# Joining the fourth sequence's last two products on TensorE at the turn, and sharing six indices of the third sequence instead of five

## What is computed

```python
def step(state, inp):
    dt_t, B_t, C_t, u_t = inp
    dA = jnp.exp(dt_t[..., None] * A)                       # (b, 2048, 16)
    state = state * dA + (dt_t * u_t)[..., None] * B_t[:, None, :]
    y = jnp.einsum('bdn,bn->bd', state, C_t)                # sum over the 16 indices n
    return (state, y)
_, ys = jax.lax.scan(step, init, xs)
y = ys.transpose(1, 0, 2) + x * D
y = y * jax.nn.silu(gate)
return y @ W_out.T
```

## Time and profile before

| | us |
|---|---|
| median of 3 runs | 2993.81 (2993.78 to 2994.83) |
| the profiled execution | 2995.75 |
| its span, first to last instruction | 2993.6 |
| PE / DVE busy | 2732.6 / 2552.1 |
| ACT / POOL busy | 1692.0 / 1925.1 |
| mean granted TensorE clock | 0.963 |

### The profile page before, as it was taken

How to read it: one execution, slowest core, us unless ns; L and a number is a source line. 1 busy time by engine, 2 the same in 40 slices (tenths; PEclk the granted TensorE clock), 3 DMA queues, 4 the chain that set the end, 5 groups by cost and what they waited for, 6 DMA issues and landing times.

```text
span 2993.6 us, 35283 instructions
## 1 busy us (share of the span) xinstructions
PE 2732.6 (91%) x11120; PEld 1562.5 (52%) x11120; DVE 2552.1 (85%) x3521; ACT 1692.0 (57%) x2848; POOL 1925.1 (64%) x884
## 2 busy tenths in 40 slices
PE   8968899999989999998999888788889999999996
PEld 4535555555555555555555455455544555555553
DVE  2259899999999999999999999999966787787785
ACT  2356566575656657565565755656534555555553
POOL 1159897888979788896988988889841222222221
PEclk9989899999999999999999999898999999999998
DMA  5432333434343343424333322432401211111110
GB/s 176 134 101 81 97 88 104 147 89 129 92 134 114 99 143 90 132 85 157 94 108 104 99 87 73 133 86 65 118 29 37 97 56 56 63 56 56 63 63 22
DMA packets 132876, 281.32 MB, mean 94 GB/s; under 512 B 12528, under 2 KB 12656, under 8 KB 132224
## 3 DMA queue, kind: packets, MB, share of 16 engines
q1 hardware_dynamic: 132736, 279.59, 30.4%
HBM read 245.86 MB, written 33.69 MB: 93 GB/s over the span
## 4 chain that ended last, share of the span: by engine, by line
PE 54%; DVE 31%; issue 9%; ACT 4%; POOL 1%; DMA 0%; DVEq 0%; ACTq 0%; POOLq 0%; SPq 0%
DVE arena L1262 17%; PE banks L473 15%; PE banks L497 9%; DVE arena L1278 7%; PE banks L567 7%; PE banks L707 4%; PE banks L660 4%; PE banks L616 3%; PE banks L641 3%; PE banks L510 2%; PE banks L671 2%; PE banks L631 2%; ACT banks L1023 2%; DVE arena L1218 1%; PE banks L714 1%
## 5 line engine op out<-in xcount | busy, mean ns | idle before, releaser
L1186 POOL TENSOR_TENSOR arena<-arena 128x2048 f32<-128x2048 f32 x256 | 1161.8, 4539 | 79.8 <-PE banks L567 79.7
L1262 DVE TENSOR_TENSOR_SCAN arena<-banks,arena 128x512 f32<-128x512 f32 x1024 | 1185.4, 1205 | 19.2 <-POOL arena L1186 16.2
L1023 ACT ACTIVATE banks<-arena,a_sb 128x508 f32<-128x508 f32 x1024 | 696.9, 684 | 734.5 <-DVE arena L1262 734.1
L473 PE MATMUL banks<-arena 128*128 128x512 f32 x2048 | 952.9, 603 | 11.0 <-DMA arena<-in_xT 8.1
L567 PEld LDWEIGHTS banks<-ident,arena 128*128 128x128 f32 x4096 | 493.6, 146 | 418.6 <-issue 197.7
L567 PE MATMUL banks<-ident,arena 128*128 128x128 f32 x4096 | 576.2, 284 | 139.4 <-DVE arena L1278 72.6
L473 PEld LDWEIGHTS banks<-arena 128*128 128x128 f32 x2048 | 373.1, 195 | 363.8 <-issue 360.5
L1278 DVE SCALAR_TENSOR_TENSOR arena<-banks,cg,arena 128x512 f32<-128x512 f32 x640 | 453.0, 739 | 72.4 <-PE banks L567 71.6
L497 PE MATMUL banks<-arena 128*128 128x512 f32 x1024 | 472.3, 600 | 5.2 <-DMA arena<-in_WoutT 3.9
L1132 POOL TENSOR_TENSOR arena<-arena 128x512 f32<-128x512 f32 x240 | 306.0, 1275 | 205.3 <-ACT arena L851 204.1
L1199 POOL TENSOR_TENSOR arena<-arena 128x512 f32<-128x512 f32 x128 | 141.2, 1103 | 434.6 <-DVE arena L1434 434.5
(11 more groups left out here) (137 smaller groups left out, 2977.1 us busy)
## 6 DMA issues: line engine op xcount, KB each, us to landing
arena<-b_scratch SPq DMA_DIRECT2D x128, 512.0 KB, 5.1
arena<-in_WinX SPq DMA_DIRECT2D x128, 256.0 KB, 2.9
arena<-in_WinZ SPq DMA_DIRECT2D x128, 256.0 KB, 2.7
arena<-in_WoutT SPq DMA_DIRECT2D x32, 1024.0 KB, 5.8
u_scratch<-arena SPq DMA_DIRECT2D x64, 256.0 KB, 5.1
arena<-u_scratch SPq DMA_DIRECT2D x16, 1024.0 KB, 9.3
arena<-x_scratch SPq DMA_DIRECT2D x32, 512.0 KB, 3.4
arena<-in_xT SPq DMA_DIRECT2D x14, 1024.0 KB, 7.9
```

The lines of the kernel that those rows point to most:

```text
L473: last = nc.tensor.matmul(home(kind, i), wr[w % 2][:, k, :], x[:, k, :], start=(k == 0), stop=(k == KC - 1))
L1023: nc.scalar.activation(by_seq(bank(i % 2))[:, :, 1:SEQ], by_seq(dt[s % 2][:, i, :])[:, :, 1:SEQ], ACT.Exp, scale=a_sb[:, QD * q + i, n:n + ...
L1186: nc.gpsimd.tensor_tensor(hb[n % 4].rearrange("p (i t) -> p i t", i=QD), dtu, brep[pair % 3][:, n % 2:n % 2 + 1, :].broadcast_to([P, QD, G ...
L1262: nc.vector.tensor_tensor_scan(h, bank(i % 2), h, 0.0, ALU.mult, ALU.add)\
```

## The change

`SHARED` gets six indices instead of five, (0, 3, 6, 8, 10, 12) for (0, 3, 6, 9, 12): VectorE makes ten products of sequence 2 per step where it made eleven, ScalarE six and GpSimd five adds for it where they were five and four. GpSimd adds sequence 3's products of indices 1 to 13 alone (SUMS = 13, where it was 15). Those of 14 and 15 stay in the two buffers of `part`; the turn waits for ScalarE's products of all 16 indices and for 13 sums, and where it transposed `acc[:, OWN, :]` it now runs three matmuls with the identity that add `acc[:, OWN, :]`, `part[:, 0, :]` and `part[:, 1, :]` in PSUM.

```diff
-SHARED = (0, 3, 6, 9, 12)
+SHARED = (0, 3, 6, 8, 10, 12)
+SUMS = N - 3
@@ pe_step, behind the loop over n
             pe.wait_ge(S["acc_ok"], KEPT * (s + 1))
-            pe.wait_ge(S["sum_ok"], (N - 1) * (s + 1))
+            pe.wait_ge(S["part_ok"], N * (s + 1))
+            pe.wait_ge(S["sum_ok"], SUMS * (s + 1))
             pe.wait_ge(S["sum2_ok"], (len(SHARED) - 1) * (s + 1))
@@
-                for b in (0, 1, OWN):
+                for b in (0, 1):
                     nc.tensor.transpose(y[:, b * P:(b + 1) * P], acc[:, b, i * P:(i + 1) * P], ident[:, :])
+                for k, v in enumerate((acc[:, OWN, :], part[:, 0, :], part[:, 1, :])):
+                    nc.tensor.matmul(y[:, OWN * P:GB * P], v[:, i * P:(i + 1) * P], ident[:, :], start=(k == 0),
+                                     stop=(k == 2))
@@ act_part
-                after(act, "sum_ok", (N - 1) * s + max(n - 2, 0))
+                after(act, "sum_ok", SUMS * s + max(n - 2, 0))
@@ pool_sums
-            if n == 0:
+            if n == 0 or n > SUMS:
                 return
             pool.wait_ge(S["part_ok"], N * s + n + 1)
-            after(pool, "sum_ok", (N - 1) * s + n - 1)
+            after(pool, "sum_ok", SUMS * s + n - 1)
```

## The result

The median of the changed kernel is 3005.99 us (3003.53 to 3006.64, 8 runs), that of the kernel before in the same comparison 2993.80: a ratio of 1.0038 with a 95% interval of 1.0029 to 1.0046, +12.2 us. The forecast was slower, 3007, so +13.2 against the 2993.81 it started from, with 2996 to 3014 as its range. The profiled execution has a span of 3004.9 us where the kernel before has 2993.6.

The account below looks back on a forecast made before the run. TensorE and VectorE were both taken as full, with TensorE setting each step's turn. Terms 7.8 - 0.5 + 0.2 + 5.5 + 0.6 = +13.6 us on the profiled 2995.75 gave 3009.3, as a median 3007, range 2996 to 3014.

Parts of the forecast that it names:

- 1, 2, 5, 6, 9: Full steps whose turn delays the next step's n = 1, where VectorE waits for TensorE: +1.3 us each.
- 4, 8: Steps followed by the layer norm on VectorE, in whose wait TensorE's +1.3 vanishes: -0.5 us for both.
- 10 to 15: Step 10 as a full step, +1.3 us; steps 11 to 15, late steps without convolution tiles from 11 on, +5.5 together.
- The matmuls: At the turn, 20 more TensorE records at 0.109 us each, covered by nothing: +2.18 us per turn.
- The wait ahead of the turn: TensorE's wait for GpSimd's last add goes: -0.53 us per full step; step 0 waited 5.06 us there.
- The bank of the second tile: Second of the turn's four banks waits for VectorE's L1291 once TensorE is early: gives back about 0.3 us.
- The sixth index: VectorE product fewer, n = 8 to 11: -0.65 us up to L510; GpSimd's later L1186 takes VectorE's gain except 0.27.
- ScalarE late at shared indices: Rival, slower: ScalarE's 0.6 us margin at n = 11 used up, 0.7 us more in ten steps, about +20; chance 0.10.
- Step 11's low clock: Step 11's turn, 4.9 us where others take 3.3, regains full clock once 2.63 us of waiting go: -1.6 us.
- The late steps give the rest back: Rival: steps 11 to 15 and 0 keep full clock, near -5 instead of +6; total +3, 2996.5 us; chance 0.15.
- Steps 3 and 7: ScalarE wait at n = 10 and 1.58 us at the turn go, the turn adds 2.18: +0.1 us each.
- VectorE sets the end of the turn: Rival, faster: VectorE's own work hides TensorE's longer turn; -10 us, 2983 to 2990; chance 0.10.

Follow-up runs that it names:

- first pair: First profiled executions of the unchanged kernel before and of the changed kernel: spans 2993.6 and 3004.9 us.
- second pair: Both kernels profiled once more without any edit: spans 2991.2 us (before) and 3004.7 us (changed).
- e4: Kernel before, with sequence 3's transpose at the turn replaced by three identity matmuls writing the same result, GpSimd's adds kept: 3026.79 us, ratio 1.0113.
- e7: Changed kernel with GpSimd's add of index 10 on one column instead of 512 (output not correct): 3001.36 us, ratio 1.0026 to before.
- e1: Changed kernel with the five old shared indices (0, 3, 6, 9, 12), so the join alone: 3002.21 us, ratio 1.0028 to before.
- e9: Changed kernel with SUMS = 14: only index 15's product joined at the turn, by two identity matmuls instead of three: 3000.45 us, ratio 1.0022 to before.
- e2: Kernel before with six shared indices (0, 3, 6, 8, 10, 12) alone, no join: 2999.97 us, ratio 1.0025.
- e5: Changed kernel with shared indices (0, 3, 5, 6, 9, 12), the sixth at n = 5, join kept: 2994.88 us, ratio 1.0007 to before.
- e8: Kernel before with shared indices (0, 3, 5, 6, 9, 12), the sixth at n = 5, no join: 2984.70 us, ratio 0.9972.
- e6: Kernel before with shared indices (0, 3, 6, 8, 10, 12), GpSimd's add of index 10 on one column (output not correct): 2980.24 us, ratio 0.9955.
- e10: Kernel before with seven shared indices (0, 3, 5, 6, 7, 9, 12), no join: 3005.11 us, ratio 1.0036.

## Why the prediction was right, and where not

The forecast for the end of step 15, +13.6, came out as +13.7 in the first pair of profiles and +12.9 in the second. That it is so near is partly luck: single terms were off by more. How much later step s leaves n = 2 of the next step (for step 15: `fin`) than the step before it did:

| steps | forecast | first pair | second pair |
|---|---|---|---|
| 0 | +0.6 | +1.4 | +2.0 |
| 1, 2, 5, 6, 9 | +6.5 | +7.9 | +7.8 |
| 4, 8 | -0.5 | -0.4 | -0.6 |
| 3, 7 | +0.2 | -2.2 | -0.7 |
| 10 to 15 | +6.8 | +7.0 | +4.4 |
| behind step 15 | 0 | -2.4 | +0.5 |
| sum | +13.6 | +11.3 | +13.4 |

- **The matmuls: right.** 20 records for 2.18 us were forecast; it is 2.22 by the full step of e4, 0.111 us a record. The Trainium skill (TensorE: Matmul & The Clock Gate, Back-to-back issue gap) has some 81 ns a matmul at 128 columns; the float32 records of this turn follow each other every 111 ns, so the trace doesn't agree for them.
- **The wait ahead of the turn: right.** It is gone in steps 1 to 15. In step 0 it shrank from 5.06 to 2.32 us, and the longer turn runs at the low clock there as was said: 7.65 us for 5.80.
- **The bank of the second tile: the right mechanism, undersized.** Forecast 0.3 us; it costs 0.45 and some 0.05 for the restart, so that the turn takes 3.12 + 2.22 + 0.50 = 5.84 us, for the 5.4 forecast. Of the 0.25 us that VectorE was to be early, 0.15 were left. This is the term that carries a full step. The second bank is 0.23 us earlier than before on the step's own axis (576.59 for 576.82), and from there to the next L568 it takes 4.06 us for 2.32: -0.23 + 1.74 = +1.51. The same two numbers give e7 (-0.63 + 1.74 = 1.11), e1 (-0.09 + 1.74 = 1.65) and e9 (-0.23 + 1.07 = 0.84).
- **The sixth index: its gain in a full step oversized, its cost elsewhere undersized.** The forecast gave it -0.65 us up to L510, then let GpSimd take most of that back. The first half is right: 0.56 us, and the wait ahead of L511 is 0.70 for the forecast 0.6. In the second half GpSimd's L1191 comes 559.87 - 2.94 - 555.73 = 1.20 us later in the step, for the 1.0 written; VectorE waits 0.68 us for it. The step that came out wrong is "DVE loses its gain there except the 0.27 us": 0.15 were left at the second bank. So with the join the index gains 0.13 us in a full step (1.65 in e1, 1.52 here). By the forecast's own terms it would be 0.35: without the index TensorE is 0.53 early, the longer first bank covers the second's lateness, and a turn costs 2.18 - 0.53 = +1.65. Over the whole kernel the index costs all the same, 3.1 us with the join (12.2 less e1's 9.1; the intervals of the two overlap) and 6.9 alone (e2).
- **ScalarE late at shared indices (a rival, 0.10): not in the full steps, but in the late ones.** No `turn(0)` of n = 9 or 11 waits for L870 in steps 1 to 10. In step 0 that of n = 9 waits 2.36 us for it. In steps 11 to 15 that of n = 11 waits 2.4 to 3.5 us for it, as here in step 12, where the earlier trace rows has 1.67 for VectorE:
```profile
1826.48 0.67 ACT L870 ACTIVATE arena<-banks,cg 128x512 f32<-128x512 f32 x1
...
1827.30 1.94 PE L568 MATMUL banks<-ident,arena 128*128 128x128 f32 x8 [2.55 <-ACT arena L870]
```
The forecast had +0.7 us for it in steps 12 to 15. Measured from the start of `turn(0)` of n = 9 to that of n = 11 it is 0.68 to 0.71 in steps 12 to 14 and 1.36 in step 15. In step 11 it came to 1.8, where the forecast had 0.9 for a cause on GpSimd and nothing for ScalarE. With the sixth index at n = 5 (e5) there is no such wait at n = 11.
- **Step 11's low clock: read from one execution.** The forecast took 1.6 us off because that turn ran at a granted clock of 0.66 behind its wait of 2.63 us. In the second profile of the kernel before the same turn stands behind the same wait and takes 3.12 us at full clock, for 4.77:
```profile
1736.06 0.52 PE L602 MATMUL banks<-ident,arena 128*128 128x128 f32 x3 [2.62 <-issue]
```
There step 14's turn takes 4.77 instead. The term is no property of the kernel, and that the first pair's +7.0 met the forecast 6.8 is luck to that extent; the second pair has +4.4.
- **The late steps give the rest back (a rival, 0.15): not so.** `turn(0)` of n = 11 takes 1.94 us in all five of steps 11 to 15 of the changed kernel, as long as at the low clock before, and these steps cost 4.4 to 7.0 us with step 10.
- **Steps 3 and 7:** the forecast had +0.1 each. Without the 1.7 us of the low clock, which no reasoning on the change could give, they are some +0.6 each in the first pair.
- **Behind step 15:** -2.4 in the first pair of profiles, +0.5 in the second: no effect of the change that two pairs could show.
- **VectorE sets the end of the turn (the rival for faster, 0.10):** half true, to the other effect. VectorE does set when the second bank begins, but the three banks behind it are TensorE's, and each is 0.56 us longer. VectorE's wait at n = 1 went from 0.54 to 2.17 us, as forecast.

**What stays open.** The steps 11 to 15 differ by up to 1.8 us each between two profiles of the kernel before, so which of their waits makes up the 4.3 us between e1 and the changed kernel in steps 11 to 14 was not isolated. The whole cost of the sixth index with the join stands there in the profiles. Nor is it settled how e8 gains 9.0 us by the medians: steps 1, 2, 4, 6, 8 and 10 give 0.4 each in its profile and steps 5 and 9 together 2.4, but 3.0 stand in steps 11 to 14, and 3.5 in steps 3 and 7, nearly all of it the clock. The same goes for most of the 20 us between e2 and e6.

## What to carry to other kernels

Moving an add from one engine into matmuls of another is priced where the work lands, record by record: here 20 records of 0.111 us on a path that had 0.54 us of waiting to lose. When a wait goes, look for the next resource in the same sequence (here the second bank) and ask which engine releases it; what was gained ahead of it is then worth nothing. And before giving an engine one operation more, look where in its queue the operation falls: a sixth index cost 7 us where its add fell into a run without idle time, and gained 9 where it stood ahead of an idle time of 3.4 us. A seventh (e10) cost it all again; there a wait of VectorE for ScalarE grew by 0.89 us.

## What the runs showed of the hardware

The same six matmuls of 512 columns in the same kernel, after the same wait of 2.0 us, ran at the full clock in one execution and partly at the low one in another, 2.74 against 4.02 us. So did a turn behind a wait of 2.6 us, 3.12 against 4.77. Steps 1, 2, 4, 6, 8 and 10 repeated to 0.03 us in the second profile of the kernel before, and yet its span was 2.4 us shorter. A single profile of each kernel can thus differ by a few microseconds for nothing, and a term of that size should be read from steps that don't touch such a place.

A float32 matmul with the identity on 128x128 took 0.222 us for its two records at the full clock, a float32 transpose 0.111 for its one.
